# A post-norm transformer layer on one core: scale operations of VectorE dropped, moved to GpSimd or given rows with holes, and layer norm operations spread over more tiles

## The reference

```python
q, k = softmax-like features of x @ Wq + bq, x @ Wk + bk      # per head of 16: exp(x - max) / (sum + eps)
v = x @ Wv + bv
ctx = (q @ k.T / (sum(q) + eps)) @ v                           # linear, so k.T @ v can be taken first
x = layernorm(x + ctx @ Wo + bo)
# FFN; fq = blockwise FP4 quantise + dequantise, blocks of 16 along the last axis:
#   scale = max(max|block| / 6, 1e-12);  fq = GRID[searchsorted(MID, |x / scale|)] * sign(x) * scale
h = silu(fq(x) @ fq(w_gate).T) * (fq(x) @ fq(w_up).T)          # 256 -> 704
x = layernorm(x + fq(h) @ fq(w_down).T)                        # 704 -> 256
```

## Time and profile before

| | |
|---|---|
| time, median of 3 runs | 774.97 us (774.73 to 778.72) |
| the profiled execution's own time | 774.18 us |
| its span | 772.2 us |
| busy: PE, PE weight loads, DVE, ACT, POOL | 720.7, 684.2, 662.2, 573.8, 575.9 us |
| granted TensorE clock, mean | 0.987 |
| attention alone, join, FFN alone, end | 0 to 266, to 330, to 747, to 772.2 us |

### The profile page before, as it was taken

One profiled execution on the slowest core, in us unless ns is written; L12 is line 12 of the kernel. 1 busy time (PEld: TensorE's weight loads), 2 busy tenths in 40 slices (PEclk: granted clock), 3 DMA queues, 4 the chain that ended last, 5 costly groups with the idle time before them and its releaser, 6 DMA issues.

```text
span 772.2 us, 17178 instructions
## 1 busy us (share of the span) xinstructions
PE 720.7 (93%) x4964; PEld 684.2 (89%) x4964; DVE 662.2 (86%) x1492; ACT 573.8 (74%) x1547; POOL 575.9 (75%) x617
## 2 busy tenths in 40 slices
PE   4999999999999978699999989999989999989984
PEld 3899998998999867599999989999989999989984
DVE  5988899889889985899899899899899898997784
ACT  3577777887887787467777767777767778778877
POOL 4677667676676675678878878888878888888861
PEclk9999999999999989899999999999999999999998
DMA  4222222222222100000000000000000000001112
GB/s 129 69 74 75 72 77 75 64 72 68 83 76 63 50 26 2 1 2 1 1 1 1 2 1 22 18 20 21 22 14 22 21 15 22 22 14 42 42 42 95
DMA packets 39768, 29.81 MB, mean 39 GB/s; under 512 B 3446, under 2 KB 39676, under 8 KB 39676
## 3 DMA queue, kind: packets, MB, share of 16 engines
q1 hardware_dynamic: 37228, 26.50, 11.4%
q10 hardware_dynamic: 2448, 2.23, 1.0%
HBM read 20.32 MB, written 8.39 MB: 37 GB/s over the span
## 4 chain that ended last, share of the span: by engine, by line
PE 47%; DVE 26%; issue 15%; POOL 5%; ACT 4%; DVEq 1%; DMA 1%; POOLq 0%; ACTq 0%; SPq 0%
PE bank L854 30%; PE wide L854 5%; POOL scratch L418 4%; DVE scratch L842 4%; PE bank L916 3%; DVE scratch L778 3%; PE bank L862 3%; DVE scratch L784 3%; DVE scratch L829 2%; PE wide L903 2%; PE bank L914 2%; PE wide L957 1%; DVE scratch L763 1%; DVE scratch L795 1%; DVE scratch L813 1%
## 5 line engine op out<-in xcount | busy, mean ns | idle before, releaser
L854 PE MATMUL bank<-wf_hi,rounded 128*128 128x352 f32 (+1 forms) x1792 | 408.6, 311 | 21.8 <-DVE rounded L835 8.3
L854 PEld LDWEIGHTS bank<-wf_hi,rounded 128*128 128x128 f32 x1792 | 301.4, 190 | 30.9 <-DVE rounded L835 14.0
L854 PE MATMUL bank<-wf_lo,rounded 128*128 128x352 f32 (+1 forms) x896 | 274.0, 306 | 0.0
L854 PEld LDWEIGHTS bank<-wf_lo,rounded 128*128 128x128 f32 x896 | 170.7, 190 | 0.0
L418 POOL TENSOR_TENSOR scratch<-scratch 128x704 f32<-128x704 f32 x64 | 93.0, 1452 | 76.6 <-DVE scratch L809 76.5
L854 PE MATMUL bank<-qkv_hi,rounded 128*128 128x512 f32 (+1 forms) x512 | 146.1, 340 | 0.0
L854 PEld LDWEIGHTS bank<-qkv_hi,rounded 128*128 128x128 f32 x512 | 93.5, 192 | 10.0
L402 POOL TENSOR_TENSOR scratch<-scratch 128x704 bf16<-128x704 f32 x64 | 98.9, 1545 | 2.2 <-ACT scratch L591 2.2
L584 ACT ACTIVATE scratch<-scratch 128x704 uint8<-128x704 f32 x64 | 50.6, 791 | 63.6 <-POOL scratch L418 63.4
L360 POOL TENSOR_TENSOR scratch<-scratch 128x512 f32<-128x512 f32 x64 | 68.1, 1064 | 36.9 <-DVE scratch L710 36.8
L425 POOL TENSOR_TENSOR scratch<-scratch 128x704 f32<-128x704 bf16 x64 | 89.1, 1392 | 5.8 <-DVE scratch L813 0.7
(11 more groups left out here) (102 smaller groups left out, 1657.7 us busy)
## 6 DMA issues: line engine op xcount, KB each, us to landing
scratch<-x_feat SPq DMA_DIRECT2D x64, 128.0 KB, 2.3
scratch<-x_tok SPq DMA_DIRECT2D x64, 128.0 KB, 2.1
out<-scratch SPq DMA_DIRECT2D x64, 128.0 KB, 1.7
scratch<-w_ffn ACTq DMA_DIRECT2D x17, 128.0 KB, 2.2
scratch<-L_attn_Wq SPq DMA_DIRECT2D x1, 256.0 KB, 3.0
scratch<-L_attn_Wk SPq DMA_DIRECT2D x1, 256.0 KB, 3.2
scratch<-L_attn_Wv SPq DMA_DIRECT2D x1, 256.0 KB, 3.9
wo<-L_attn_Wo SPq DMA_DIRECT2D x1, 256.0 KB, 3.1
```

The lines of the kernel that those rows point to most:

```text
L854: last = pe.matmul(dst, x(c), w(c), start=first and n == 0, stop=n == len(terms) - 1)
```

## The change

LN_A goes from four batches of 16 tiles to batches of 32, 16 and 16; LN_B from 16, 16, 16, 8, 4, 4 to 32, 16, 8, 4, 4. Each batch has a pace, the operations in one tile: 2 (slots 1 and 5), 4 (slots 0, 2, 4, 6) or 7 (all). `ready` starts the normalisations when a batch is done at its pace and spreads them up to the start of the next. The scales without SHY go: `e_sc` (VectorE, L804) and `bsc` (GpSimd, L420) are dropped, `xq` and `hq` are multiplied by `e_s2` and `bs2`, and the weights' scale is divided by SHY instead. `e_s2` moves from VectorE (L778) to GpSimd, behind `hq` in even tiles, with three buffers; `e_inv` moves from even to odd tiles. `bs2` is laid out as 11 rows of 4 with a row step of 5.

```diff
-LN_A = ((0, 16), (16, 16), (32, 16), (48, 16))
-LN_B = ((0, 16), (16, 16), (32, 16), (48, 8), (56, 4), (60, 4))
+LN_SLOTS = {2: (1, 5), 3: (0, 3, 6), 4: (0, 2, 4, 6), 7: (0, 1, 2, 3, 4, 5, 6)}
+LN_A = ((0, 32, 2), (32, 16, 2), (48, 16, 4))
+LN_B = ((0, 32, 2), (32, 16, 2), (48, 8, 4), (56, 4, 7), (60, 4, 7))
...
-        bmx, bsc, bs2, binv = ([part(NB) for _ in range(2)] for _ in range(4))
+        bmx, binv = ([part(NB) for _ in range(2)] for _ in range(2))
+        bs2 = [part(11 * (NB // 11 + 1)).rearrange("p (a b) -> p a b", a=11)[:, :, 0:NB // 11] for _ in range(2)]
...
         def ready(m, batches, lag):
-            spans = [count for _, count in batches[1:]] + [batches[-1][1]]
-            return [(g, first + k) for g, (first, count) in enumerate(batches) for k in range(count)
-                    if first + count + lag + 2 + k * spans[g] // count == m]
+            starts = [first + count + lag + -(-LN_OPS // pace) for first, count, pace in batches]
+            spans = [later - start for start, later in zip(starts, starts[1:])] + [batches[-1][1]]
+            return [(g, first + k) for g, (first, count, _) in enumerate(batches) for k in range(count)
+                    if starts[g] + k * spans[g] // count == m]
+
+        def ln_ops(k, m, batches, lag):
+            for g, (first, count, pace) in enumerate(batches):
+                slots = LN_SLOTS[pace]
+                if k in slots:
+                    at = slots.index(k) + pace * (m - first - count - lag)
+                    if 0 <= at < LN_OPS:
+                        yield at, g
...
GpSimd, FFN step:
-                        need(pool, e_scs, p + 1)
                         pool.tensor_tensor(blocks(xq[:, s * D:(s + 1) * D]), blocks(e_g[e][:, half]),
-                                           over(e_sc[e][:, scales], XB), ALU.mult).then_inc(x_q, 1)
+                                           over(e_s2[p % 3][:, scales], XB), ALU.mult).then_inc(x_q, 1)
...
-                        pool.tensor_scalar(bsc[b1], bmx[b1], 1.0 / 6.0, TINY, ALU.mult, ALU.max).then_inc(h_sc, 1)
                     if live(i, t, -2):
-                        need(pool, h_sc, m - 1)
                         need(pool, h_t, m - 3)
                         need(pool, h_g, m - 1)
-                        pool.tensor_tensor(blocks(hq[b][:, 0:I]), blocks(hg[b]), over(bsc[b], NB),
+                        pool.tensor_tensor(hq[b][:, 0:I].rearrange("p (a c e) -> p a c e", a=11, e=BLK),
+                                           hg[b].rearrange("p (a c e) -> p a c e", a=11, e=BLK),
+                                           bs2[b].unsqueeze(3).broadcast_to((P, 11, NB // 11, BLK)),
                                            ALU.mult).then_inc(h_q, 1)
+                    if t % 2 == 0 and live(i, t, 6):
+                        p, e = pair(i, t, 6)
+                        need(pool, e_max, p + 1)
+                        need(pool, e_invs, p - 2)
+                        need(pool, x_q, 2 * (p - 2))
+                        pool.tensor_scalar(e_s2[p % 3], e_mx[e], SHY / 6.0, TINY * SHY, ALU.mult, ALU.max).then_inc(e_s2s, 1)
...
VectorE, FFN step (the e_s2 and e_sc operations and the even e_inv are taken out):
+                    if odd and live(i, t, 5):
+                        p, e = pair(i, t, 5)
+                        need(dve, e_s2s, p + 1)
+                        need(dve, e_xns, p - 1)
+                        dve.reciprocal(e_inv[e], e_s2[p % 3]).then_inc(e_invs, 1)
                     if odd and live(i, t, 3):
                         p, e = pair(i, t, 3)
                         need(dve, e_mgs, p + 1)
...
                     if live(i, t, -1):
                         need(dve, h_max, 2 * m)
                         need(dve, h_inv, m - 2)
+                        need(dve, h_q, m - 2)
                         dve.tensor_scalar(bs2[b1], bmx[b1], SHY / 6.0, TINY * SHY, ALU.mult, ALU.max).then_inc(h_s2, 1)
```

More of the change, by code:

```diff
@@ L84, in layer_kernel @@
         nbias = sb("nbias", [P, NT])
[L85 to L88, removed]
+        ln_v = sb("ln_v", [P, 8 * T])
+        ln_h = sb("ln_h", [P, 8 * T], U32)
+        ln_t = sb("ln_t", [P, 8 * T])
+        ln_u = sb("ln_u", [P, 8 * T])
         ident = sb("ident", [P, P])
@@ L159, in layer_kernel @@
         e_mg, e_c, e_g = ([part(D, BF16) for _ in range(2)] for _ in range(3))
-        e_mx, e_sc, e_s2, e_inv = ([part(2 * XB) for _ in range(2)] for _ in range(4))
+        e_mx, e_inv = ([part(2 * XB) for _ in range(2)] for _ in range(2))
+        e_s2 = [part(2 * XB) for _ in range(3)]
         xq = part(T * D)
@@ L206, in layer_kernel @@
             sem(f"a_{k}") for k in "post qhi qlo kvm c chi clo out res sm nm sq ln x1".split())
[L207 to L208 removed]
+        e_max, e_s2s, e_invs, e_xns, e_ys, e_mgs, e_cs, e_gs, x_q = (
+            sem(f"e_{k}") for k in "max s2 inv xn y mg c g q".split())
         x_t, x_hi, x_lo = sem("x_t"), sem("x_hi"), sem("x_lo")
[L210 removed]
+        gu_a, gu_b, si_a, si_b, h_a, h_b, h_max, h_s2, h_inv, h_xn, h_y, h_mg, h_c, h_g, h_q = (
             sem(f"b_{k}") for k in
[L212 removed]
+            "gua gub sia sib ha hb hmax hs2 hinv hxn hy hmg hc hg hq".split())
         h_t, h_hi, h_lo, d_s, y_s, y_sm, y_nm, y_sq, y_ln, y_o = (
@@ L612, in layer_norm @@
             def layer_norm(k, g, batches, norm, done, sq):
-                n, count = batches[g]
+                n, count, _ = batches[g]
                 at = slice(n, n + count)
@@ L644, in ln @@
                     def ln(k):
[L645 to L648, removed]
+                        for at, g in ln_ops(k, m, LN_A, A_LN):
+                            layer_norm(at, g, LN_A, 0, a_ln, a_sq)
                     def q_lo():
@@ L689, in attention @@
                         need(dve, w_qs, i)
[L690 removed]
+                        dve.tensor_scalar(w_sc, w_mx, 1.0 / (6.0 * SHY), TINY / SHY, ALU.mult, ALU.max).then_inc(w_scs, 1)
                     if live(i, t, -1):
@@ L751, in ln @@
                     def ln(k):
[L752 to L755, removed]
+                        for at, g in ln_ops(k, m, LN_B, B_LN):
+                            layer_norm(at, g, LN_B, 1, y_ln, y_sq)
                     if even and live(i, t, 6):
@@ L773, in ffn @@
                                           ALU.add).then_inc(y_s, 1)
[L774 to L777, removed]
-                        dve.tensor_scalar(e_s2[e], e_mx[e], SHY / 6.0, TINY * SHY, ALU.mult,
-                                          ALU.max).then_inc(e_s2s, 1)
                     if live(i, t, -1):
                         need(dve, h_b, m)
-                        need(dve, h_sc, m - 2)
                         need(dve, h_s2, m - 2)
@@ L794, in ffn @@
                         need(dve, h_inv, m - 2)
+                        need(dve, h_q, m - 2)
                         dve.tensor_scalar(bs2[b1], bmx[b1], SHY / 6.0, TINY * SHY, ALU.mult, ALU.max).then_inc(h_s2, 1)
-                    if even and live(i, t, 6):
-                        p, e = pair(i, t, 6)
-                        need(dve, e_s2s, p + 1)
-                        need(dve, e_xns, p - 1)
-                        dve.reciprocal(e_inv[e], e_s2[e]).then_inc(e_invs, 1)
-                    if odd and live(i, t, 3):
-                        p, e = pair(i, t, 3)
-                        need(dve, x_q, 2 * (p - 1))
-                        dve.tensor_scalar(e_sc[e], e_mx[e], 1.0 / 6.0, TINY, ALU.mult, ALU.max).then_inc(e_scs, 1)
                     ln(2)
```

2 lines of the change are left out of this document (removed).

## The result

The changed kernel takes 763.24 us, median of 4 runs (763.04 to 764.19), beside 774.85 us for the kernel before (774.29 to 778.72): a ratio of 0.984, 95% interval 0.9815 to 0.9865. In a later comparison of five rounds it took 763.22 us (763.00 to 765.41). The profiled execution took 763.37 us with a span of 761.6 us, 10.6 us under the span before. The forecast was 760.0 us, with a range of 754 to 769. In that later comparison the kernel before took 778.23 us, and the ratio was 0.983 [0.980, 0.985]: the kernel before comes at two levels, near 774.5 and near 778 us, of which more under "Even batches", and its profile is of the lower one. Four executions, three of them of the kernel before, took 1198 to 2774 us and are left out.

What follows compares the result with a forecast made beforehand. TensorE bounds, late where GpSimd holds VectorE in the FFN loop and layer norm. Gains 6.1 + 6.6 + 2.3 + 0.5 - 0.5 = 15.0; 774.2 - 15.0 + 0.8 = 760.0 us, range 754 to 769.

Steps and rivals of the forecast that it cites:

- The FFN: 58 FFN tiles stood 15.7 us above TensorE's pace; 6.1 was to go in ordinary pairs and 6.6 in layer norm batches.
- the loop: Chain of waits in ordinary FFN pairs: moving L778 and dropping L804 and L420 brings TensorE's pace, gaining 6.1 us.
- layer norm: FFN layer norm batches cost 9.6 us before; spread, 1.5 per batch, 3.0 in all: gain 6.6, between -3.0 and 9.6.
- rival B: FFN loop gets no shorter, as L791 and L842 take up the holds L778 leaves: 766 us, chance 0.12.
- Rival A: Spread layer norm operations are held nearly everywhere; both FFN batches lose 5 to 6.3 us: 769 us, chance 0.17.
- Attention: Three attention stretches with layer norm lose 3.1 us; a residue of 0.8 (0 to 3.1) stays: gain 2.3.
- just enough: Attention tiles 47 to 62: doubled normalisation adds 2.0 us of ScalarE per four tiles, against its wait of 2.04.
- The join: TensorE's wait for wf_lo shortens by 0.5 and L778's going gives 0.4, against later e_xn: +0.5 us, from -2 to 3.5.
- of which little reaches TensorE: In the join, e_xn waits for the later e_inv, making attention features 1.5 us late, with little effect on TensorE.
- The end: L420's going gives 0.4, but bunched normalisations in tiles 61 to 67 cost more: -0.5 us, from -1.5 to 0.8.
- Rival D: Doubled normalisation on ScalarE delays FFN tiles 45 to 60, attention 47 to 62 and 61 to 65: 780 us, chance 0.05.
- Rival E: bs2 with holes still waits and L425 slows by a quarter; TensorE's transposes wait for hq: 766 us, chance 0.05.

Runs made afterwards that it cites:

- Even batches: Changed kernel with layer norm batches of 16 tiles (later ones 8, 4, 4) at paces 2, 2, 2, 7 and 2, 2, 4, 7, 7, 7; 763.10 us against 763.22.
- the scale part: Kernel before with the changed scale operations, layer norm batches and pace as before: 773.76 us, ratio 0.998 to the kernel before.
- with the gap kept: Scale operations changed, old layer norm batches, plus an unused one-input GpSimd operation of 44 elements: 767.75 us, ratio 0.991 to the kernel before.
- layer norm only: Kernel before with the new layer norm batches and pace, scale operations untouched: 778.43 us, ratio 1.002 to the kernel before.

## Why the prediction was right, and where it was not

*The FFN: 12.7 forecast, 13.4 measured, but not as two terms.* The prediction took 6.1 for the loop and 6.6 for layer norm, as if each stood alone. The loop fell to TensorE's pace as worked out (pairs of 13.70), e_s2 on GpSimd takes 0.32 (0.36 taken), L842's successor and e_inv did not fill the room (rival B is out), and the two pace-2 batches cost 0.5 each where 1.5 was taken (the pace-4 batch at the start costs 1.8, where nothing was). Rival A is out too: held operations are there, one in two, and the room covers them. But alone the parts give -0.1 and 1.5 of FFN time, together 13.4. The first needs the second, because dropping L420 closed the gap through which the dense operations went: with the gap kept it gives 8.0 alone. The second gives more with the first: layer norm loses 6.5 us of FFN time with the old scale operations and 2.8 with the new, and the ordinary pairs, which in layer norm only lose 7.7 us, lose nothing without L778. That VectorE's room is the reason is argued; no run changed the room alone. The prediction saw that slot 5 would meet L425 without L420 ahead of it and priced it for the spread batches; it never asked for the price of L420 with the dense ones, and of its rivals none said that the terms depend on each other. The experiments' expectation of 768 us for the scale part failed by 6 us for that reason. That of 771 for the layer norm part failed by 7 mostly elsewhere, in the join and the end.

*Attention: 2.3 forecast, 1.7 measured.* By stretches 3.1 us of loss became 1.7 (0.12, 0.13, 0.36, 0.37, 0.69), where a residue of 0.8 was taken; another 0.2 was gained before the first stretch. Of the three stretches of layer norm the first went to 16.39 and the second to 16.51, but the third only from 17.46 to 17.08. In the two at 16.74 and 16.76 the loss is the doubled normalisation's, which the prediction had at "just enough": even batches take it away. ScalarE's wait before L517 (now L535), which was to be near zero there, is 1.25 us.

*The join: +0.5 forecast, -3.3 measured.* This is the step that failed. With the matmul time that the low clock cost taken off, the join is 58.9 before and 58.0 after, +0.9, so that the sum of the waits came out near the forecast. VectorE reached wf_lo 0.6 us sooner (0.5 taken), and e_xn waited 1.31 for e_inv (1.5 taken). Not foreseen was that e_s2 too waits for VectorE in GpSimd's queue and makes the features behind it 1.6 us late. And "of which little reaches TensorE" left out the clock: 4.1 us more of matmul time went to 1.2 GHz. How much of the 3.3 us that is can't be told from one pair of executions; the two of even batches had 2.95 us of join for 3.55 of such time. The trace of before had the rows for it (rows of 2 us with 0.50 to 0.67 behind waits of 1.06 and 1.46 us, and rows at 1.00 behind waits of 1.81 and 1.24 at 302 and 306 us), and the prediction did not weigh them.

*The end: -0.5 forecast, -1.2 measured*, within its bounds (-1.5 to 0.8). The chain there goes through ScalarE's normalisations, which rows 10 had two at a time:

```profile
742.39 1.08 ACT scratch L488 x2
...
746.39 1.08 ACT scratch L488 x2
...
750.38 1.08 ACT scratch L488 x2
```

With even batches the end is 29.6 again. Rival D was this in small, and the 0.36 of two attention stretches too; in the FFN it did not happen.

*Rival E.* The holes do nothing for the time and bs2 isn't held, with them or without, and L435 with its pattern of four dimensions takes 1.39 us as L425 did: no loss. The two-port rule that the prediction took for them was not put to the test.

Sum: 13.4 + 1.7 - 3.3 - 1.2 = 10.6 us of span, against 15.0 forecast; the difference of 4.4 is the join (3.8), attention and the end (1.3), less 0.7 from the FFN. The median missed by 3.2 only, because the 0.8 us that were added for the median of the kernel before didn't come with the changed kernel (763.24, its profiled execution 763.37): that much of the small miss is luck.

## What to carry to other kernels

When two engines share something, an operation taken off one of them can also take away the gap through which the other worked: look at what ran in the shadow of what you drop, and price two edits together and apart. A wait in a place where TensorE is already thinly used can cost the work behind it at the lower clock besides its own length, in one execution and not in the next: read the granted clock of that stretch before you call a microsecond of delay small. A hold that is seen on an engine is no cost until that engine's room is used up.

## What the runs showed of the hardware

GpSimd operations over 704 elements with two inputs held VectorE's small layer norm operations to their very end: these took up to 1.5 us instead of 0.16 and ended 0.01 to 0.06 us behind them. An operation of 0.16 us that started 0.14 us ahead of such a GpSimd operation was not held. One kernel, on identical instructions, loses 5.5 or 9.0 us of matmul time to the clock of 1.2 GHz in the same 70 us, from one execution to the next, and a wait of TensorE of 2.40 us in the same place was followed by the full clock in one kernel's execution and by half of it in another's. The kernel before comes near 774.5 us with a mean clock of 0.985 or more and near 778 with 0.981 or less.
